# A graph network's last layer on one core: one neighbour sum and one transpose per graph, in one stack

## The reference, cut to what matters

```python
# layer 2
y = jnp.matmul(adj_matrix, x) + x          # x here is h
y = jnp.matmul(y, weight) + bias           # weight: 64 x 64
# ... row norm, batch norm over all graphs, relu
# layer 3
messages = jnp.einsum('bij,bjh->bih', adjacency, h)
node_in = jnp.concatenate([h, messages], axis=-1)
dh = jnp.tanh(node_in @ W1 + b1) @ W2 + b2       # W1: 128 x 64, W2: 64 x 64
```

## Time and profile before

| | |
|---|---|
| device time, median of 3 runs | 1490.96 us (1490.86 to 1496.52) |
| profiled execution, own time | 1490.96 us |
| its span | 1489.0 us |
| instructions | 41572 |
| PE busy, share of the span | 1322.7 us (89%) |
| DVE busy | 1171.4 us (79%) |
| ACT busy | 1113.2 us (75%) |
| layer 3, first matmul to the end of the span | 1404.62 us to 1489.0 us |

### The profile page before, as it was taken

How to read it: one execution, slowest core, us unless ns; L and a number is a source line. 1 busy time by engine, 2 the same in 40 slices (tenths; PEclk the granted TensorE clock), 3 DMA queues, 4 the chain that set the end, 5 groups by cost and what they waited for, 6 DMA issues and landing times. The chain is left out here.

```text
span 1489.0 us, 41572 instructions
## 1 busy us (share of the span) xinstructions
PE 1322.7 (89%) x11243; PEld 1077.9 (72%) x11244; DVE 1171.4 (79%) x3091; ACT 1113.2 (75%) x2424; POOL 496.4 (33%) x611
## 2 busy tenths in 40 slices
PE   0799999999999999999999999997999997972298
PEld 0477777777777777777777777775888887920298
DVE  6598898988888889888898898985444445978755
ACT  0788888888888888888888888883555554916676
POOL 0143344443343344443343344442112221057400
PEclk9999999999999999999999999998999998986599
DMA  7000000000000000000000000000000000000022
GB/s 150 15 9 9 15 7 7 7 13 8 7 7 7 14 7 7 7 13 9 7 7 7 14 7 7 0 2 1 1 0 0 0 0 0 0 1 0 2 55 56
DMA packets 40926, 18.11 MB, mean 12 GB/s; under 512 B 19573, under 2 KB 40887, under 8 KB 40887
## 3 DMA queue, kind: packets, MB, share of 16 engines
q1 hardware_dynamic: 40354, 17.42, 4.8%
q10 hardware_dynamic: 532, 0.21, 0.1%
HBM read 13.44 MB, written 4.19 MB: 12 GB/s over the span
## 5 line engine op out<-in xcount | busy, mean ns | idle before, releaser
L833 DVE SCALAR_TENSOR_TENSOR acc<-slot_banks,acc 128x768 f32<-128x768 f32 x512 | 486.7, 951 | 43.0 <-PE slot_banks L555 32.5
L901 POOL TENSOR_TENSOR acc<-acc 128x384 f32<-128x384 f32 x128 | 128.2, 1002 | 562.2 <-DVE onediff L827 557.6
L555 PE MATMUL slot_banks<-ac_hi,work 128*128 128x192 f16 x1408 | 264.4, 246 | 1.0 <-ACT slot_banks L719 1.0
L555 PE MATMUL slot_banks<-ac_lo,work 128*128 128x192 f16 x1408 | 263.9, 246 | 0.0
L555 PE MATMUL slot_banks<-ac_hi,onediff 128*128 128x192 f16 x1024 | 186.1, 247 | 19.2 <-DVE acc L833 15.1
L555 PE MATMUL slot_banks<-ac_lo,onediff 128*128 128x192 f16 x1024 | 184.9, 246 | 0.0
L555 PEld LDWEIGHTS slot_banks<-ac_hi,work 128*128 (+1 forms) x1408 | 137.3, 98 | 62.5 <-issue 43.4
L555 PEld LDWEIGHTS slot_banks<-ac_lo,work 128*128 (+1 forms) x1408 | 138.0, 98 | 14.9 <-issue 6.3
L815 DVE TENSOR_SCALAR work<-work,slot_key 128x1024 f16 x256 | 119.6, 478 | 25.8 <-issue 25.8
L712 ACT ACTIVATE work<-slot_banks 128x576 f32<-128x576 f32 x128 | 83.4, 651 | 68.9 <-PE slot_banks L555 68.9
L555 PEld LDWEIGHTS slot_banks<-ac_hi,onediff 128*128 x1024 | 104.0, 102 | 41.4 <-issue 38.1
(11 more groups left out here) (261 smaller groups left out, 3308.5 us busy)
## 6 DMA issues: line engine op xcount, KB each, us to landing
adj_in<-in_adj_dram SPq DMA_DIRECT2D x32, 256.0 KB, 2.8
out_dram<-acc SPq DMA_DIRECT2D x32, 128.0 KB, 2.0
l1w<-in_L_gnn_W_dram SPq DMA_DIRECT2D x2, 64.0 KB
l1b<-in_L_gnn_b_dram SPq DMA_DIRECT2D x2, 64.0 KB
x_all<-in_x_dram SPq DMA_DIRECT2D x4, 0.2 KB, 12.1
nm_in<-in_nodemask_dram ACTq DMA_DIRECT2D x1, 64.0 KB
w1a<-in_L_gnn_W_dram ACTq DMA_DIRECT2D x1, 48.0 KB
w1b<-in_L_gnn_W_dram ACTq DMA_DIRECT2D x1, 48.0 KB
```

What stands on the lines that cost most here:

```text
L555: last = nc.tensor.matmul(unit(pair, t, 1), hot(t), part[:, q, H:2 * H].unsqueeze(1), start=False, stop=(e == 1 and (t % SB == SB - 1 or t ...
L833: nc.vector.scalar_tensor_tensor(out=sums, in0=unit((q + k) % 2, 0, SU), scalar=0.0, in1=sums, op0=ALU.min, op1=ALU.add).then_inc(s_free[k ...
L901: nc.gpsimd.tensor_tensor(acc[:, q, 0:2 * H], acc[:, q, 0:2 * H], acc[:, q, 2 * H:4 * H], ALU.add)
```

## The change

The slots become (1, 3, 4, 6): zero, graph 0, zero, graph 1, graph 2, zero, graph 3. In layer 3, each graph now has its own 128 columns of the bank: a matmul with the weights [what stands before the graph's slot, graph] puts the sums on partitions 64 to 127, and a transpose of the graph's 64 columns then writes h itself over partitions 0 to 63 of the same columns. So `msg` holds, for each graph, h over the sums, which is the transpose of `node_in`. The hidden layer multiplies it by W1 as it is: `l3w1` is 192 columns wide, [zero, W1, zero]; for graphs 0 and 2 the columns [W1, zero] are the weights, for graphs 1 and 3 [zero, W1], and the two results are accumulated, stacked on the partitions as before. `l3wa`, `l3wb` and `l3wd` go, with five loads; `l3w1` and `l3w1b` have two. In layer 2 the sums are now stacked graph 0 first, and the blocks of `l2w` stand on the diagonal. Of the loads 20 are left of 23.

```diff
-        SLOT = (1, 2, 4, 5)
+        SLOT = (1, 3, 4, 6)
...
-            (l2w[0:F, F:2 * F], a["L2_gnn_weight"]), (l2w[F:2 * F, 0:F], a["L2_gnn_weight"]),
+            (l2w[0:F, 0:F], a["L2_gnn_weight"]), (l2w[F:2 * F, F:2 * F], a["L2_gnn_weight"]),
...
-            (l3wa[0:F, 0:F], a["L3_gnn_W1"][0:F, :]), (l3wa[F:2 * F, F:2 * F], a["L3_gnn_W1"][0:F, :]),
-            (l3wb[0:F, F:2 * F], a["L3_gnn_W1"][F:2 * F, :]), (l3wb[F:2 * F, 0:F], a["L3_gnn_W1"][F:2 * F, :]),
-            (l3wd[:, :], a["L3_gnn_W1"][F:2 * F, :]),
+            (l3w1[:, F:2 * F], a["L3_gnn_W1"]), (l3w1b[:, :], a["L3_gnn_W1"][F:2 * F, :]),
...
-                for m in (l3wa, l3w2):
+                for m in (l2w, l3w2):
                     v.memset(m[0:F, F:2 * F], 0.0)
                     v.memset(m[F:2 * F, 0:F], 0.0)
-                for m in (l2w, l3wb):
-                    v.memset(m[0:F, 0:F], 0.0)
-                    v.memset(m[F:2 * F, F:2 * F], 0.0)
+                v.memset(l3w1[:, 0:F], 0.0)
+                v.memset(l3w1[:, 2 * F:3 * F], 0.0)
...
-                nc.vector.tensor_tensor(l3wa[0:F, 0:F], l3wa[0:F, 0:F], l3wd[:, :], ALU.subtract)
-                nc.vector.tensor_tensor(l3wa[F:2 * F, F:2 * F], l3wa[F:2 * F, F:2 * F], l3wb[F:2 * F, 0:F], ALU.subtract)
+                nc.vector.tensor_tensor(l3w1[0:F, F:2 * F], l3w1[0:F, F:2 * F], l3w1b[:, :], ALU.subtract)
...
-                        first = (SLOT[q] - 1 + odd) * F
+                        first = (SLOT[q] - odd) * F
...
                     for q in range(GS):
-                        odd = q % 2
-                        first = (SLOT[q] - 1 + odd) * F
-                        nc.tensor.matmul(ps[:, (q // 2) * N:(q // 2 + 1) * N], hn[:, u, first:first + 2 * F],
-                                         adjT[:, ds((GS * grp(u, i) + q) * N, N)], start=(odd == 0), stop=(odd == 1))
-                    for t in range(GS // 2):
-                        first = SLOT[2 * t] * F
-                        last = nc.tensor.transpose(ps[:, (2 + t) * N:(3 + t) * N], hn[:, u, first:first + 2 * F],
-                                                   ident[:, :])
+                        cols = slice(q * N, (q + 1) * N)
+                        at = SLOT[q] * F
+                        nc.tensor.matmul(ps[:, cols], hn[:, u, at - F:at + F],
+                                         adjT[:, ds((GS * grp(u, i) + q) * N, N)], start=True, stop=True)
+                        last = nc.tensor.transpose(ps[0:F, cols], hn[:, u, at:at + F], ident[:, :])
...
-                    nc.tensor.matmul(bank[4 * u + 1][:, 0:2 * N], l3wb[:, :], msg[:, u, 0:2 * N], start=True, stop=False)
-                    nc.tensor.matmul(bank[4 * u + 1][:, 0:2 * N], l3wa[:, :], msg[:, u, 2 * N:4 * N],
-                                     start=False, stop=True).then_inc(s_lin3[u], 1)
+                    sums = msg[:, u, :].rearrange("p (t e j) -> p e t j", t=2, e=2)
+                    for odd in range(2):
+                        last = nc.tensor.matmul(bank[4 * u + 1][:, 0:2 * N].rearrange("p (t j) -> p t j", t=2),
+                                                l3w1[:, (1 - odd) * F:(3 - odd) * F], sums[:, odd],
+                                                start=(odd == 0), stop=(odd == 1))
+                    last.then_inc(s_lin3[u], 1)
```

More of the change, by code:

```diff
@@ L94, in gnn_stack_kernel @@
         beta = sb("beta", [N, F])
-        l3wa = sb("l3wa", [2 * F, 2 * F])
-        l3wb = sb("l3wb", [2 * F, 2 * F])
-        l3wd = sb("l3wd", [F, F])
+        l3w1 = sb("l3w1", [2 * F, 3 * F])
+        l3w1b = sb("l3w1b", [F, F])
         l3b1 = sb("l3b1", [2 * F, 1])
```

## The result

| | before | changed |
|---|---|---|
| median | 1493.88 us (6 runs, 1490.86 to 1496.52) | 1501.81 us (6 runs, 1499.54 to 1503.28) |
| profiled execution, own time | 1490.96 us | 1501.28 us |
| its span | 1489.0 us | 1499.6 us |

The ratio is 1.0055, with a 95% interval of 1.0039 to 1.0073: slower, by 5.8 to 10.9 us. The forecast was 1497.9 us and a range to 1500.5; the time is outside it. The two profiled executions differ by 10.3 us, more than the medians (7.9 us).

A forecast was written before the change was run, and what follows sets the result against it. The prediction took TensorE's pace to bound layer 3, at 2.42 us per group of four graphs. It summed 1490.96 + 6.98 = 1497.94 us, all other terms taken as nothing, with a range of 1496.0 to 1500.5 us.

The forecast's parts named there:

- The transposes: Layer 3 on TensorE: two more 64-column transposes per group, 64 in all at 0.109 us each, adding 6.98 us.
- The passes between the transposes: Layer 3 aggregation: 256 matmul passes now alternating with transposes; a possible 0.67 us given back, taken as nothing.
- the hidden layer's new operands: Layer 3 hidden layer: moving operand in two runs, weights sliced from a wider tile; at most 0.4 us, taken as nothing.
- Width changes: Layer 3, rival: 256 changes between 128 and 64 weight columns each cost time, giving 1500.5 to 1540 us; chance 0.08.
- The clock as a rival: Layer 3: transposes count less as work, so the 1.2 GHz stretch repeats, +2.5 us, 1500.4 us; chance 0.04.
- The loads and memsets at the start: Kernel start: three fewer loads and two fewer memsets, covered by VectorE's 6.25 us wait for x; taken as nothing.
- the base: Whole kernel: the profiled execution's own time, 1490.96 us, also the median of three runs, to which added time was summed.

The follow-up runs named there:

- b_extra: The kernel before with two more 64-column transposes per group of layer 3, into an unused bank, output unused: 1497.52 us, ratio 1.0050.
- a_warm: The changed kernel with unread matmuls keeping TensorE busy between layer 2 and layer 3: 1495.98 us, ratio 1.0031 against the kernel before.
- b_warm: The kernel before with unread matmuls keeping TensorE busy between layer 2 and layer 3: 1489.20 us, ratio 0.9967 against the kernel before.
- a_grouped: The changed kernel with each layer 3 group's four sums first, then its four transposes: 1502.17 us, ratio 1.0070 against the kernel before.
- a_twice: The changed kernel with every transpose of layer 3 issued twice: 1515.83 us, ratio 1.0159 against the kernel before.

## Why the prediction was wrong

- The transposes. 64 x 0.109 = 6.98 us. Layer 3 grew by 7.11 us, in the isolated form by 6.85 (b_extra) and 6.76 us (a_warm against b_warm). Right, with a unit of 106 to 107 ns instead of 109.
- The passes between the transposes, and the hidden layer's new operands: taken as nothing, 0.01 us per group by the rows above. Right. Width changes: rival, 0.08, refused by a_grouped. The Trainium skill's sentence that changing the tiling mode drains the engine ("TensorEngine Tiling (Array Packing)", Key Properties) does not bear on such a pair: either 64 columns of weights are no such mode, or the drain is too short to see here (under 2 ns per change).
- The clock as a rival (transposes not counted as work): layer 3 has 1.00 from 1420 us on, in a_twice too, with eight transposes per group. Not seen in any run.
- **The first step that failed, a term put at nothing: "The loads and memsets at the start ... Nothing."** The memsets' time was indeed covered by the wait for x, and layer 0 opens as before (the last instruction ahead of it at 36.37 us, before 36.44). But an instruction removed also shortens the program. The two memsets less moved VectorE's stall at the end of layer 0 by two instructions, and it went from 1 us to 2.8 us. I had looked for what covers the removed instructions, not for what stands behind them in the stream. The earlier trace rows shows only the start; the 0.98 us of idleness ahead of L743, which no producer explains, was in the same trace, and I had not looked at it. (A reading beside it was off too, without effect: from the end of SyncE's last issue, 34.88 us, to L264's start, 36.44, it is 1.56 us, and 1.8 only to L264's end.)
- Given back and lost again. The 2.40 us at layer 1 were 0.88 us at batch norm and 3.44 us at layer 3, with 6.8 us more of batch norm at 1.2 GHz. My sum took everything ahead of layer 3 as fixed. That the added 2.56 us come from the stall is not shown: both lengths of batch norm occur with short and with long stalls.
- **The second step that failed, and the larger part of the miss: the base.** I set the sum on 1490.96 us, the median of three runs, and gave the range no term for its spread. Three more runs made the median 1493.88, and beside the experiments it was 1490.67, 1492.80, 1492.44 and 1492.64, in a spread of 1489.6 to 1496.7. Of the 3.9 us between forecast and result, 2.9 are this base. The rest, 7.93 - 6.98 = 0.95 us in the medians, is what may be left there of the late start, but the interval of 5.8 to 10.9 us holds 6.98 as well. The spread goes with each run's mean granted clock: of the 70 runs of before beside the experiments, those at 0.970 took 1489.6 to 1493.0 us, those at 0.968 1492.9 to 1494.8, and those at 0.965 1495.9 to 1496.7. Why the clock differs between runs of one kernel, no run shows. The profiled execution of before was one at 0.970.

The base alone put the time out of the range: with 1493.88 the sum would have been 1500.9 us. With the transposes alone the difference is 6.85 us, as b_extra shows. The forecast that the change falls just within half a per cent was narrow, and the ratio says 0.55%, with 0.47% inside its interval.

## What to carry to other kernels

A transpose on TensorE costs what its moving operand costs, 128 fp32 columns 106 to 109 ns, whether it turns 64 columns or 128; pack it full. When instructions are taken from an engine's stream, or added, look for idle stretches behind them that no producer explains: here the stretch stayed at its place in the program, and another instruction came to stand there. To settle microseconds in a kernel whose runs spread over seven, compare runs at the same mean granted clock. And give a forecast of an absolute time the spread of the base as a term of its own.

## What the runs showed of the hardware

VectorE's stall at a fixed place in its program (ahead of its 5122nd instruction in the trace, register instructions counted, in all fourteen traces): 0.9 to 1.1 us in all five profiles with the base count of memsets, 3.1 to 3.3 us in all six with two fewer (with 0.4 us that stand there anyway), 1.52 us in both with three more and 2.67 us with eight more. The Trainium skill, "Runtime: NRT & Kernel Launch", Instruction fetch mechanics, says that an engine's instructions are brought in by blocks while it executes, that crossing a block is mostly hidden and that a taken branch to a target outside the fetched blocks breaks it. That fits the fixed place, 5 us behind the last branch instruction before it (971.4 us in the trace of before); that it is mostly hidden does not hold here. The traces tie the stall to such a transfer. In all fourteen, it ends 1.8 to 2.0 us after the start of one transfer of 8 KB on the queue q14, which carries instructions: 975.21 and 977.05 us before, 977.70 and 979.48 changed, and there is none on q14 in the 790 us ahead of it. With the stall short, the transfer starts before VectorE runs dry (by 0.8 to 0.9 us, or 0.3 with three more memsets); with it long, 0.8 to 1.1 us after. So the length is set by when that transfer starts; what starts it stays open.

Unread matmuls in TensorE's waits, some 220 of them, cost nothing that could be seen and gave 3.6 us, by keeping 2.4 GHz from batch norm into layer 3.
